# Four graph layers over 64 pairs: the loop of every engine written out, and the last constants made before the third step

## The reference

```python
x0   = x                                            # (128, 128, 256)
h    = relu(layernorm(x0))
qkv  = (h @ w_qkv)                                  # 8 heads of 32
attn = softmax(where(adj == 0, -inf, q @ k.T * 32**-0.5))
o    = (attn @ v) @ w_proj + b_proj
x1   = x0 + o + layernorm(o) * ln_gamma + ln_beta
h    = relu(layernorm(x1))
rel  = adj.T * (h @ Wq.T @ (h @ Wk.T).T)
x2   = x1 + (rel / norm(rel, axis=2)) @ (h @ Wv.T)
h    = relu(layernorm(x2));  hw = h @ W
e    = leaky_relu(hw @ a1 + (hw @ a2).T, 0.2) * adj
x3   = x2 + elu(softmax(e) @ hw + beta * hw)
h    = relu(layernorm(x3))
out  = x3 + (adj @ h) @ weight + bias
```

## Time and profile before

| | us |
|---|---|
| median of 3 runs | 1529.49 (1529.12 to 1531.04) |
| the profiled execution | 1527.43 |
| its span, first to last instruction | 1525.4 |
| PE busy | 1482.7 (97%) |
| DVE busy | 1301.0 (85%) |
| ACT busy | 1120.1 (73%) |
| POOL busy | 661.3 (43%) |
| granted TensorE clock, mean | 0.994 |

### The profile page before, as it was taken

How to read it: one execution, slowest core, us unless ns; L and a number is a source line. 1 busy time by engine, 2 the same in 40 slices (tenths; PEclk the granted TensorE clock), 3 DMA queues, 4 the chain that set the end, 5 groups by cost and what they waited for, 6 DMA issues and landing times.

```text
span 1525.4 us, 46270 instructions
## 1 busy us (share of the span) xinstructions
PE 1482.7 (97%) x16392; PEld 1375.0 (90%) x16392; DVE 1301.0 (85%) x3726; ACT 1120.1 (73%) x2884; POOL 661.3 (43%) x981
## 2 busy tenths in 40 slices
PE   6989999999999999999989999999999999999996
PEld 5879999999999999999989999999999999999985
DVE  3888888888888888888888898898898898898895
ACT  4667777777777777777767777777777777777763
POOL 2244444444444444444444444444444444444442
PEclk9999999999999999999999999999999999999999
DMA  3000010000000010000010010010000010000001
GB/s 107 15 16 15 23 30 22 23 29 22 23 30 22 23 29 22 23 29 23 23 31 18 28 29 18 27 30 18 28 30 19 26 30 20 25 29 22 17 16 35
DMA packets 38102, 39.84 MB, mean 26 GB/s; under 512 B 2416, under 2 KB 37488, under 8 KB 37872
## 3 DMA queue, kind: packets, MB, share of 16 engines
q1 hardware_dynamic: 37872, 36.84, 7.9%
HBM read 20.05 MB, written 16.78 MB: 24 GB/s over the span
## 4 chain that ended last, share of the span: by engine, by line
PE 94%; DVE 2%; issue 2%; ACT 1%; POOL 1%; DMA 0%; POOLq 0%; DVEq 0%; ACTq 0%
PE bank L325 41%; PE mid L360 7%; PE mid L325 6%; PE mid L372 5%; PE bank L384 4%; PE mid L388 4%; PE mid L365 4%; PE mid L446 4%; PE mid L534 4%; PE mid L423 4%; PE bank L341 3%; PE bank L474 3%; PE mid L341 2%; PE mid L452 1%; PE bank L458 1%
## 5 line engine op out<-in xcount | busy, mean ns | idle before, releaser
L557 ACT ACTIVATE probs<-mid,neg_max 128x128 f32<-128x128 f32 x1024 | 295.3, 423 | 49.9 <-DVE neg_max L797 49.9
L897 POOL TENSOR_TENSOR rstd<-var_eps,minus_half 128x2 f32<-128x2 f32 x320 | 244.0, 763 | 25.1
L927 POOL TENSOR_TENSOR xb<-x,b_proj_beta 128x512 f32<-128x512 f32 x64 | 82.7, 1293 | 283.1 <-DVE o_res L807 283.1
L895 POOL TENSOR_TENSOR var_eps<-mean_var,eps 128x2 f32<-128x2 f32 x320 | 104.2, 326 | 167.1 <-DVE mean_var L717 167.1
L912 POOL TENSOR_TENSOR inv_norm<-sum_sq,minus_half 128x2 f32<-128x2 f32 x64 | 44.1, 689 | 260.8 <-DVE sum_sq L772 260.8
L730 DVE SCALAR_TENSOR_TENSOR h_t_lo<-bank,h_t_hi 128x512 fp32r<-128x512 f32 x128 | 88.4, 691 | 79.1 <-ACT h_t_hi L650 55.4
L713 DVE BATCH_NORM_STATS2 stats<-x 128x6 f32<-128x256 f32 x384 | 143.3, 414 | 5.8 <-DMA x<-in_x 3.6
L360 PE MATMUL mid<-ident,probs 128*128 128x128 f32 x1024 | 144.0, 275 | 3.7 <-ACT probs L557 3.7
L724 DVE TENSOR_SCALAR z<-x,mean_var,rstd 128x256 f32<-128x256 f32 x384 | 141.2, 410 | 2.7 <-POOL rstd L897 2.7
L360 PEld LDWEIGHTS mid<-ident,probs 128*128 128x128 f32 x1024 | 117.7, 142 | 4.8 <-ACT probs L557 4.8
L384 PE MATMUL bank<-probs_t,v 128*32 128x128 f32 x2048 | 105.9, 278 | 6.6 <-issue 6.0
(11 more groups left out here) (149 smaller groups left out, 5649.5 us busy)
## 6 DMA issues: line engine op xcount, KB each, us to landing
x<-in_x SPq DMA_DIRECT2D x64, 256.0 KB, 2.7
out_x<-x SPq DMA_DIRECT2D x64, 256.0 KB, 2.2
w_qkv_sb<-in_w_qkv SPq DMA_DIRECT2D x1, 768.0 KB, 4.5
w_q_sb<-in_w_q SPq DMA_DIRECT2D x1, 256.0 KB, 4.4
w_k_sb<-in_w_k SPq DMA_DIRECT2D x1, 256.0 KB, 4.7
w_v_sb<-in_w_v_t SPq DMA_DIRECT2D x1, 256.0 KB, 5.6
w_proj_sb<-in_w_proj SPq DMA_DIRECT2D x1, 256.0 KB, 5.8
w_gat_x<-in_w_gat SPq DMA_DIRECT2D x1, 256.0 KB, 6.1
```

What stands on the lines that cost most here:

```text
L557: last = act.activation(probs[:, r, s], mid[:, r, s * N:(s + 1) * N], ACT.Exp, bias=neg_max[:, r, s:s + 1])
L895: pool.tensor_tensor(var_eps[:, k], mean_var[:, k, :, 1], eps[:], ALU.add).then_inc(ln_eps[k], 1)
L897: pool.tensor_tensor(rstd[:, k], var_eps[:, k], minus_half[:], ALU.pow).then_inc(ln_rstd[k], 1)
L927: pool.tensor_tensor(xb[:], x0[:, i1], both(b_proj_beta), ALU.add).then_inc(xb_ready, 1)
```

## The change

Nothing of the computation changes. Three things do:

1. `run` has no `Fori` any more: on PE, ACT, DVE and POOL all 71 steps are written out. With it the wait values are constants everywhere, and the helpers lose their second form.
2. SP's loop is written out in the same way; its DMAs have constant addresses.
3. `last_constants` of DVE and of POOL stand ahead of step 2 in place of step 5. The wait of PE (`last_weights`) stays ahead of step 5, and the DMAs that bring the late constants stay where they are.

`bank_free`, the helper for waits that a PSUM bank be free, now leaves out all but the first of its waits wherever all its readers have a pair, also in the first and last steps; in steps 8 to 63 it did so before.

```diff
@@ run
-            for t in range(FIRST):
+            for t in range(PAIRS + STREAMS - 1):
                 for made_by, make in set_up:
                     if made_by == t:
                         make()
-                step(t, t % 2, streams(t))
-            with eng.Fori(FIRST, PAIRS - STEPS + 1, STEPS) as t:
-                for i in range(STEPS):
-                    step(t + i if i else t, i % 2, [True] * STREAMS)
-            for t in range(PAIRS, PAIRS + STREAMS - 1):
                 step(t, t % 2, streams(t))
...
@@ bank_free
-            if isinstance(readers[0][1], int):
-                for s, p, n in readers:
-                    if p >= 0:
-                        eng.wait_ge(s, done(min(p, PAIRS - 1), n))
-            else:
-                s, p, n = readers[0]
-                eng.wait_ge(s, done(p, n))
+            if all(0 <= p < PAIRS for _, p, _ in readers):
+                readers = readers[:1]
+            for s, p, n in readers:
+                if p >= 0:
+                    eng.wait_ge(s, done(min(p, PAIRS - 1), n))
...
@@ SP
-            LAST = PAIRS - 2
-            for t in range(FIRST):
-                step(t, t % 2, t >= 1, t >= 7)
-            with sp.Fori(FIRST, LAST - 1, 2) as t:
-                step(t, 0, True, True)
-                step(t + 1, 1, True, True)
-            for t in range(LAST, PAIRS + 7):
-                step(t, t % 2, t - 1 + 2 < PAIRS, True)
+            for t in range(PAIRS + 7):
+                step(t, t % 2, 1 <= t < PAIRS + 1 - 2, t >= 7)
...
@@ VectorE
-            run(dve, step, [(1, first_constants), (2, next_constants), (5, last_constants)])
+            run(dve, step, [(1, first_constants), (2, next_constants), (2, last_constants)])
...
@@ GpSimd
-            run(pool, step, [(1, next_constants), (5, last_constants)])
+            run(pool, step, [(1, next_constants), (2, last_constants)])
```

More of the change, by code:

```diff
@@ L28, in gnn_stack @@
     STREAMS = 8
-    STEPS = 28
-    FIRST = STREAMS + (PAIRS - STREAMS) % STEPS
     x_pairs = x.rearrange("(t b) n d -> t n b d", b=2)
@@ L213, in wait_before @@
         def wait_before(eng, s, p, n=1):
-            if not isinstance(p, int) or p > 0:
+            if p > 0:
                 eng.wait_ge(s, p * n)
         def wait_two_before(eng, s, p):
-            if not isinstance(p, int) or p > 1:
+            if p > 1:
                 eng.wait_ge(s, p - 1)
         def bank_free(eng, *readers):
-            if isinstance(readers[0][1], int):
-                for s, p, n in readers:
-                    if p >= 0:
-                        eng.wait_ge(s, done(min(p, PAIRS - 1), n))
-            else:
-                s, p, n = readers[0]
-                eng.wait_ge(s, done(p, n))
+            if all(0 <= p < PAIRS for _, p, _ in readers):
[3 more added lines that the diff above has]
+                    eng.wait_ge(s, done(min(p, PAIRS - 1), n))
         def streams(t):
@@ L294, in step @@
                 pb, p_out = t - 1, t - 7
-                peeled = isinstance(t, int)
                 if load:
@@ L299, in step @@
                     sp.wait_ge(xb_ready, done(pb))
-                    sp.dma_start(x0[:, i], x_pairs[pb + 2] if peeled else x_pairs[bass.ds(pb + 2, 1)][0])\
-                      .then_inc(x_in[i], 16)
+                    sp.dma_start(x0[:, i], x_pairs[pb + 2]).then_inc(x_in[i], 16)
                 if store:
@@ L304, in step @@
                     sp.wait_ge(x4_ready, done(p_out))
-                    sp.dma_start(out_pairs[p_out] if peeled else out_pairs[bass.ds(p_out, 1)][0], x4[:, i])\
-                      .then_inc(x_out[i], 16)
-            LAST = PAIRS - 2
-            for t in range(FIRST):
-                step(t, t % 2, t >= 1, t >= 7)
-            with sp.Fori(FIRST, LAST - 1, 2) as t:
-                step(t, 0, True, True)
-                step(t + 1, 1, True, True)
-            for t in range(LAST, PAIRS + 7):
-                step(t, t % 2, t - 1 + 2 < PAIRS, True)
+                    sp.dma_start(out_pairs[p_out], x4[:, i]).then_inc(x_out[i], 16)
+            for t in range(PAIRS + 7):
+                step(t, t % 2, 1 <= t < PAIRS + 1 - 2, t >= 7)
             for i in range(2):
@@ L850, in step @@
                     dve.wait_ge(x3b_ready, done(p7))
-                    if not isinstance(t, int) or p7 > 1:
+                    if p7 > 1:
                         dve.wait_ge(x_out[i7], 8 * (p7 - i7))
                     dve.tensor_tensor(x4[:, i7], pair_rows(y_bank), x3b[:], ALU.add).then_inc(x4_ready, 1)
-            run(dve, step, [(1, first_constants), (2, next_constants), (5, last_constants)])
+            run(dve, step, [(1, first_constants), (2, next_constants), (2, last_constants)])
         @block.gpsimd
```

## The result

| | before | changed |
|---|---|---|
| median of 6 runs, us | 1529.24 (1526.72 to 1531.04) | 1515.08 (1513.97 to 1515.72) |
| the profiled execution, us | 1527.43 | 1514.17 |
| its span, us | 1525.4 | 1512.4 |

The changed kernel takes 0.9909 of the time before, 95% interval 0.9896 to 0.9922: 14.2 us less by the medians, 13.3 us by the profiled executions, 13.0 us by their spans. Forecast were 1516.6 us in a range of 1514.0 to 1520.3 and a span of 1512.5.

A forecast was written before the change was run, and what follows sets the result against it. PE, busy for 97% of the span, was taken as the bound. Savings of 8.34 us (last constants) and 4.56 us (loop), 12.90 together, took the median from 1529.49 to 1516.6 us, range 1514.0 to 1520.3.

The forecast's parts named there:

- two odd stretches: Between the scores of steps 4 and 5 (27.79 us) and of steps 35 and 36 (27.42 us); full stretches take 22.86.
- The last constants, old place: Ahead of step 5: pause and lower clock cost 8.34 us, all saved; the stretch of step 4 falls to 19.45 us.
- the 6.01 us: PE's standstill between steps 4 and 5, read as a wait for `last_weights`.
- that rival: Ahead of step 5 another wait is close behind `last_weights`; in the limit only 4.56 us gained, 1524.9 us; chance 0.03.
- The last constants, new place: Ahead of step 2 on POOL and DVE: they fit into idle time and cost 0 us.
- The lower bound: DVE's two score reductions beside POOL's weight splits are not held up: 0 us, as for reduction L794.
- the upper one: Each of those two reductions is held up like an L842, by 1023 ns: 2.0 us together; as a rival, chance 0.05.
- The slack: Time to spare behind the moved constants ahead of step 2: 8.4 us on POOL, 3.1 us on DVE.
- The loop: PE's jump back, stretch of step 35 to 36: pauses of 2.66 and 1.22 us; 4.56 us saved by writing out.
- the slower rival: Straight code starves PE, up to 4.56 us each time; three cases eat up the gain, four give 1534.8 us; chance 0.03.
- no change: Whole kernel: the jump cost and the wait at step 5 are both replaced, 1529.5 us; chance 0.02.
- my list of what can move: In the tail PE runs at 1.2 GHz for a while; where that falls may shift the time 2.2 us either way.

The follow-up runs named there:

- the constants alone: The kernel before with only the last constants of VectorE and GpSimd moved ahead of step 2, all loops kept: 1520.27 us against 1529.57.
- the short body: The kernel before with a loop body of 14 steps in place of 28, so three jumps back in place of one: 1543.28 us against 1529.57.
- the head moved: The changed kernel with PE alone looping, over steps 12 to 37 in place of 8 to 35: 1518.74 us.
- PE's loop alone: The changed kernel, but PE alone keeps the loop of 28 steps; ACT, DVE, POOL and SP are written out: 1519.37 us.

## Why the prediction was right

**The bound.** PE was the bound and its two odd stretches were the whole lever. The other 56 full stretches came out unchanged, and writing out the loops of the other engines gave nothing (1515.33 us with them kept, 1515.08 without).

**The last constants, old place.** Forecast 8.34 us with a stretch of 19.45; measured 8.28 with 19.51, and 8.34 with the constants alone. The reading of the 6.01 us, put down to "issue", as `last_weights` held, and the two shares moved one at a time showed its inner order: GpSimd holds up VectorE, and VectorE then holds up PE. Nothing else was late behind it, so that rival is out.

**The last constants, new place.** Forecast 0, measured 0. The one open price was that of the reductions beside the splits. The lower bound was right, 1.22 and 1.21 us, and the upper one, from L842, described other instructions: wa_prod paid it when it was moved to step 3. The slack was real but narrow: one step later it was gone, at a cost of 3.3 us.

**The loop.** Forecast 4.56 us, measured 4.55; no stall in written-out code; 57 instruction blocks in 618 us as before. My reasons held for this jump. But I wrote "up to 4.56 us" of each stall in the slower rival, and that bound was wrong: the same kind of jump took 5.9 to 8.4 us with the short body. With three such stalls that rival would have been past no change and not at it. It did not come, since straight code did not stall at all.

**The sum.** The span came out at 1512.4 us against 1512.5, but partly by luck: the start was 1.5 us shorter and the tail 1.4 us longer. Only the tail's part was in my list of what can move. By the medians the saving was 14.2 us, not 12.9. The median of before stands on executions 1.8 us longer than the profiled one, and I assumed that what they have more stays. Some of it went: the kernel before spreads over 4.3 us, the changed one over 1.8. The longer executions have the lower clock; which stretch holds it is open.

## What to carry to other kernels

Where one engine is the bound, cut the span at a mark that comes once a step and compare the stretches: the two that stood out gave both terms of the sum within 0.1 us, clock included. One-time work in a filling pipeline belongs where every engine that makes it idles, and where its parts on VectorE and GpSimd don't overlap; that the consumer's wait is later isn't enough. A jump of the bound engine costs some microseconds, once for each time it is taken (3.0 to 8.4 here), and pauses in the drain can cost one or two more through TensorE's clock.

## What the runs showed of the hardware

- A taken branch of PE to far code: a pause of 2.2 to 2.7 us in five profiles, 3.7 to 4.0 us where another block was already being fetched, and a second pause of up to 1.8 us with the loop's head of 28 steps, none with the head moved. The Trainium skill (Runtime: NRT & Kernel Launch, section Instruction fetch mechanics) says that a taken branch out of the window stalls until the target's instructions are fetched, and these pauses agree. The two profiles of the kernel before share it out differently, 2.66 and 1.22 us in the first, and in the second

```profile
794.29 1.13 PE L423 MATMUL mid<-hw,att_t 128*128 128x256 f32 x4 [2.15 <-issue]
...
797.76 0.30 PE L388 MATMUL mid<-probs_t,ones 128*32 128x128 f32 x2 [1.78 <-issue]
```

- Where the clock fell behind this jump, the stretch was hardly longer than where it did not: 27.41 us (constants alone) and 27.73 (PE's loop alone) against 27.42 and 27.48 in the two profiles of before. With the constants alone PE at 1.2 GHz took L423 in 2.07 in place of 1.13 us, and the second pause shrank from 1.22 to 0.11 us. What fits is that the arrival of the second block set the end either way.

```profile
785.21 2.07 PE L423 MATMUL mid<-hw,att_t 128*128 128x256 f32 x4 [2.40 <-issue]
```

- The first 18.5 to 20.2 us differ between profiles of the same instructions. The fold (old L398) takes 3.64 us before and 3.10 in the changed kernel. Behind it the same products take 0.41 us each up to the scores in the one, and 0.28 us from 16.7 us on in the other, although the profile has the clock of the start at 1.00 in the first and 0.91 in the second. So the granted clock of the first microseconds does not tell PE's pace. Why the pace differs is open. Before, then changed:

```profile
17.28 0.41 PE L325 MATMUL mid<-h_t_lo,w_qkv_hi 128*128 128x256 f32 x1
```

```profile
17.28 0.28 PE L308 MATMUL mid<-h_t_lo,w_qkv_hi 128*128 128x256 f32 x1
```
